# Routed experts on Trainium2: slots and ends formed by TensorE, rank rows for three experts, fetches by row block

## The reference, cut to what matters

```python
logits = xn @ router_weight.T + router_bias        # 8192 tokens, 16 experts
probs = softmax(logits, axis=-1)
_, idx = top_k(logits.T, 512)                      # each expert takes its 512 best tokens
xe = xn[idx]
h = gelu(einsum('ecd,efd->ecf', xe, fc1_weight) + fc1_bias[:, None, :])
y = einsum('ecf,edf->ecd', h, fc2_weight) + fc2_bias[:, None, :]
gates = take_along_axis(probs.T, idx, axis=1)
output = zeros.at[idx.reshape(-1)].add((y * gates[:, :, None]).reshape(-1, d))
```

## Time and profile before

| | |
|---|---|
| median of 3 runs | 966.09 us (965.4 to 966.34) |
| profiled execution | 965.09 us, span 963.4 us |
| mean granted clock of TensorE | 0.939 |
| PE busy | 855.3 us (89%), 6159 matmuls |
| DVE busy | 741.0 us (77%) |
| POOL busy | 593.4 us (62%) |
| ACT busy | 510.5 us (53%) |

### The profile page before, as it was taken

The page is one execution under the profiler, slowest core; times in us unless marked ns, Lnnn a source line. Parts: engine busy times, 40 slices in busy tenths (PEclk is TensorE's granted clock), DMA queues, the critical chain, the costliest instruction groups (busy, mean ns, idle before and its releaser), DMA issues. The chain is left out here.

```text
span 963.4 us, 21098 instructions
## 1 busy us (share of the span) xinstructions
PE 855.3 (89%) x6159; PEld 732.4 (76%) x6159; DVE 741.0 (77%) x1662; ACT 510.5 (53%) x929; POOL 593.4 (62%) x567
## 2 busy tenths in 40 slices
PE   8799999999999999999811159999999999999995
PEld 7678888788878887887611147989999999999985
DVE  4588888888888888887599766888777777777642
ACT  3456655665566556655366127465555555555541
POOL 4157666766676667665552356688877766775344
PEclk9899999999999999999855569999999999999998
DMA  5456665666566666654241033466665666665333
GB/s 174 153 196 202 217 215 201 206 214 222 198 201 218 211 201 207 219 200 150 86 146 44 14 103 122 157 176 174 167 166 158 162 160 163 166 173 147 93 71 44
DMA packets 129510, 156.51 MB, mean 162 GB/s; under 512 B 22449, under 2 KB 104625, under 8 KB 129345
## 3 DMA queue, kind: packets, MB, share of 16 engines
q1 hardware_dynamic: 104064, 113.05, 36.3%
q0 software_dynamic: 15616, 25.70, 12.5%
q10 hardware_dynamic: 9792, 17.31, 4.9%
HBM read 74.93 MB, written 26.28 MB: 105 GB/s over the span
## 5 line engine op out<-in xcount | busy, mean ns | idle before, releaser
L599 DVE TENSOR_REDUCE NM<-bank 128x4 f32<-128x480 f32 x256 | 155.5, 650 | 61.1 <-PE bank L761 61.0
L424 ACT ACTIVATE PT<-bank 120x512 f32<-120x512 f32 x256 | 142.5, 603 | 36.1 <-PE bank L786 34.9
L348 POOL TENSOR_SCALAR XN<-X,mv,rstd 128x256 f32<-128x256 f32 x124 | 150.5, 1222 | 14.1 <-POOL rstd L343 13.3
L1691 PE MATMUL bank<-W2H,HH 128*128 128x256 f32 x512 | 144.7, 283 | 2.0 <-issue 2.0
L1693 PE MATMUL bank<-W2H,HL 128*128 128x256 f32 x512 | 143.6, 280 | 0.0
L1692 PE MATMUL bank<-W2L,HH 128*128 128x256 f32 x512 | 143.5, 280 | 0.0
L1147 POOL DMA_INDIRECT out_dram<-C,IO x60 | 111.9, 1865 | 50.6 <-issue 31.3
L1417 DVE TENSOR_TENSOR HL<-hf,HH 128x512 fp32r<-128x512 f32 x128 | 87.3, 690 | 50.6 <-ACT HH L1572 49.9
L786 PE MATMUL bank<-QX,KX 128*120 128x256 f32 x512 | 110.6, 309 | 8.8 <-DMA QX<-NMT 5.2
L557 DVE RECIPROCAL RR<-RC 128x256 f32<-128x256 f32 x64 | 111.4, 1742 | 5.4 <-DMA RC<-PVS 5.3
L1567 ACT ACTIVATE hf<-bank,B 128x512 f32<-128x512 f32 x128 | 87.8, 686 | 41.4 <-PE bank L1693 35.5
(11 more groups left out here) (198 smaller groups left out, 1909.8 us busy)
## 6 DMA issues: line engine op xcount, KB each, us to landing
QX<-QH ACTq DMA_DIRECT2D x64, 256.0 KB
W<-w1T_dram SPq DMA_DIRECT2D x16, 1024.0 KB, 5.6
W<-w2T_dram SPq DMA_DIRECT2D x16, 1024.0 KB
X<-x_dram SPq DMA_DIRECT2D x32, 256.0 KB, 3.1
QX<-QL SPq DMA_DIRECT2D x32, 256.0 KB
XB<-x_dram SPq DMA_DIRECT2D x32, 256.0 KB, 2.9
RC<-PVS SPq DMA_DIRECT2D x64, 128.0 KB, 2.1
OC<-PVS SPq DMA_DIRECT2D x64, 128.0 KB, 2.2
```

Of the source, the lines that this page charges most:

```text
L348: ins = pool.tensor_scalar(dst[:, t, :], src[:, t, :], mv[:, t, 0:1], rstd[:, t:t + 1], ALU.subtract, ALU.mult)
L424: act.activation(PT[u][0:M, HE * k:HE * (k + 1), :], score_bank(b, k // 2)[k % 2][0:M, :], ACT.Exp, scale=SCALE) \
L599: dve.tensor_reduce(NM[u][:, t, :].rearrange("p (f n e) -> p n e f", n=HN, e=HE)[:, n, :, :], smax_bank[q % 2][:, 0:4 * M].rearrange("p (e ...
L1691: pe.matmul(o, wh, xh, start=first, stop=False)
```

## The change

TensorE now forms the ends of experts 2 to 15 by eight fp32 matmuls of a prefix column with the identity, and the slots (chosen and transposed in one) by sixteen: a prefix block times the identity, and the block shifted by one times its negative. prefix moves by one element in its tile, so that base, the value ahead of the first token, fits before it. Lines 1467 and 1468 and the larger spread_of go; minus_ident is new on POOL. FE is 3: expert 2's rank rows also come from first_ranks, and each store has its own semaphore. find_first and the first gathers work by halves of two row blocks. columns(0, 0) stands ahead of the counts of expert 1, tiles(1) ahead of those of expert 0, tiles(2) goes into the second loop of lows. The reciprocal moves behind spread_of. POOL's landed waits go, and its order becomes: first_lookup and first_gather of 0, 1, 2, first_rows 0, ranks(1, 1), first_rows 1, ranks(1, 0), gather(1, 1), ranks(2, 0).

The core of the diff (declarations, and what only renames, are left out):

```diff
@@ -1094,10 +1099,10 @@
         sp.wait_ge(prefix_ready, 1)
         for e in range(FE):
             sp.dma_start(first_ranks.rearrange("(e c j) p -> e c (j p)", e=FE, c=NC)[e], prefix[e:P:E, :]) \
-                .then_inc(first_stored, 16)
+                .then_inc(first_stored[e], 16)
         sp.wait_ge(table_ready, 1)
         rows = table_rows.rearrange("p j s q -> p (j s q)")
-        for e in (2, 0, 1, 3):
+        for e in range(4):
             sp.dma_start(slot_table.rearrange("(e c j) w -> e c (j w)", e=E, c=NC)[e], rows[e:P:E, :]).then_inc(early_stored, 16)
         for c in range(NC):
             sp.dma_start(slot_table.rearrange("(e c j) w -> c e (j w)", e=E, c=NC)[c, 4:E, :], rows[E * c + 4:E * (c + 1), :]) \
...
@@ -1171,32 +1177,34 @@
         pool.wait_ge(rsm_ready, 1)
         pool.tensor_tensor(probs[:, :, :], expl, rsm[:, :, :].to_broadcast([P, NT, E]), ALU.mult).then_inc(probs_ready, 1)
 
-        pool.wait_ge(first_stored, 16 * FE)
-        pool.wait_ge(row_ready, 1)
-
-        def landed(done, count):
-            pool.wait_ge(done, 16 * GT * count)
-
-        lookup(FR[0], first_ranks, row_of[:, 0, :], first_ranked[0])
-        lookup(FR[1], first_ranks, row_of[:, 1, :], first_ranked[1], range(GT // 2))
-        pool.wait_ge(idx_ready, 1)
-        lookup(XG[0], xn_table, II[0], gathered[0])
-        lookup(FR[1], first_ranks, row_of[:, 1, :], first_ranked[1], range(GT // 2, GT))
-        pool.wait_ge(idx_ready, 2)
-        lookup(XG[1], xn_table, II[1], gathered[1])
+        def first_lookup(e):
+            pool.wait_ge(first_stored[e], 16)
+            pool.wait_ge(row_ready, 1 + e // 2)
+            pool.wait_ge(idx_ready, e - 1) if e > 1 else None
+            for g in range(GT):
+                lookup(FR[e % 2], first_ranks, row_of[:, e, :], first_ranked[g], (g,))
+
+        def first_gather(e):
+            for half in range(2):
+                pool.wait_ge(half_found, 2 * e + half + 1)
+                if e == 2:
+                    pool.wait_ge(xt_done, 1)
+                lookup(XG[e % 2], xn_table, II[e % 2], gathered[e % 2], range(2 * half, 2 * half + 2))
+
+        first_lookup(0)
+        first_gather(0)
+        first_lookup(1)
+        first_gather(1)
+        first_lookup(2)
+        first_gather(2)
         pool.wait_ge(early_stored, 64)
-        pool.wait_ge(probs_ready, 1)
-        landed(gathered[1], 1)
+        lookup(first_rows[0], slot_table, row_of[:, 0, :], first_gated[0])
+        ranks(1, 1)
+        lookup(first_rows[1], slot_table, row_of[:, 1, :], first_gated[1])
         ranks(1, 0)
-        landed(ranked[0], 1)
-        lookup(first_rows[0], slot_table, row_of[:, 0, :], first_gated[0])
-        landed(first_gated[0], 1)
-        lookup(first_rows[1], slot_table, row_of[:, 1, :], first_gated[1])
-        gather(1, 0)
-        ranks(1, 1)
+        gather(1, 1)
         pool.wait_ge(slot_stored, 16 * NC)
         ranks(2, 0)
-        gather(1, 1)
         ranks(2, 1)
         add_up(0, 0, True)
         gather(2, 0)
...
@@ -1270,8 +1278,6 @@
                 decide(turn, r)
         decide(0, 30, True)
         n[0] = BASE + 2 * 31
-        dve.wait_ge(sum_ready, 4)
-        dve.reciprocal(rsm[:, :, :], tree[3]).then_inc(rsm_ready, 1)
         thr = cand[:, :].bitcast(FP32)
         dve.tensor_scalar(gt, LT, thr, None, ALU.is_gt, ALU.add, accum_out=counts[:, 0:1]).then_inc(step_dve, 1)
         dve.tensor_scalar(eq, LT, thr, None, ALU.is_equal, ALU.add, accum_out=counts[:, 1:2]).then_inc(step_dve, 1)
...
@@ -1284,6 +1290,7 @@
         dve.tensor_scalar(need[:, 4:5], need[:, 2:3], need[:, 0:1], float(CAP), ALU.subtract, ALU.add).then_inc(need_ready, 1)
         dve.tensor_tensor(need[:, 5:6], need[:, 2:3], need[:, 3:4], ALU.add).then_inc(need_ready, 1)
         dve.wait_ge(need_ready, 2)
+        dve.tensor_tensor(base, need[:, 5:6], need[:, 4:5], ALU.min)
         then(dve.tensor_tensor_scan(eq_count, eq, zero_row[:, :], need[:, 5:6], ALU.add, ALU.add))
         dve.scalar_tensor_tensor(prefix, eq_count, need[:, 4:5], gt_count, ALU.min, ALU.add).then_inc(prefix_ready, 1)
 
...
@@ -1294,8 +1301,13 @@
                               prefix[:, P - 1:CT:P].rearrange("p (a b j) -> p a b j", a=1, b=1).to_broadcast([P, hi - lo, NC, TC]),
                               ALU.mult).then_inc(spread_ready, 1)
 
-        def ends_of(lo, hi, src):
-            dve.tensor_copy(ends[:, lo:hi, :], src.rearrange("p (e t) -> p e t", t=NT)).then_inc(ends_ready, 1)
+        def first_ends():
+            dve.tensor_copy(ends[:, 0:2, :], first_ends_bank[:, 0:2 * NT].rearrange("p (e t) -> p e t", t=NT)).then_inc(ends_ready, 1)
+
+        def other_ends(k):
+            js = TC // 2
+            dve.tensor_copy(ends[:, 2:E, :].rearrange("p e (c j) -> p j e c", j=TC)[:, js * k:js * (k + 1), :, :].rearrange("p j e c -> p e c j"),
+                            ends_bank[k][:, 0:js * NC * (E - 2)].rearrange("p (j c e) -> p e c j", j=js, c=NC)).then_inc(ends_ready, 1)
 
         def tiles(g):
             lo, hi = GROUPS[g]
...
@@ -1357,11 +1369,19 @@
             dve.wait_ge(gate_picked, e + 1)
             dve.tensor_copy(all_gates[:, bass.ds(e, 1), :].rearrange("p o r -> p (o r)"), G[u][:, :]).then_inc(gate_found, 1)
 
-        def find_first(u):
-            dve.wait_ge(first_ranked[u], 16 * GT)
-            count(u, FR, first_place, range(GT))
-            dve.wait_ge(place_ready, u + 1)
-            numbers(u, u, first_place)
+        def find_first(e, half):
+            u, at, gs = e % 2, (first_place if e < 2 else place), slice(2 * half, 2 * half + 2)
+            for g in range(2 * half, 2 * half + 2):
+                dve.wait_ge(first_ranked[g], 16 * (e + 1))
+                ins = dve.tensor_scalar(before[:, g, :], FR[u][:, g, :], s_col[:, g:g + 1], None, ALU.is_le, ALU.add,
+                                        accum_out=at[u][:, g:g + 1])
+            ins.then_inc(half_counted, 1)
+            dve.wait_ge(half_counted, 2 * e + half + 1)
+            if e == 2:
+                dve.wait_ge(gathered[0], 16 * GT)
+            dve.scalar_tensor_tensor(II[u][:, gs], at[u][:, gs], float(NT), tile_of[:, e, gs], ALU.mult, ALU.add).then_inc(half_found, 1)
+            if half:
+                dve.scalar_tensor_tensor(out_row[:, e, :], tile_of[:, e, :], float(P), at[u][:, :], ALU.mult, ALU.add).then_inc(idx_ready, 1)
 
         def pick_first(u):
             dve.wait_ge(first_gated[u], 16 * GT)
...
@@ -1375,7 +1395,7 @@
             count(u, RK, place, (r,))
             if r == GT - 1:
                 dve.wait_ge(gathered[u], 16 * GT * i)
-                dve.wait_ge(place_ready, 2 * i + u + 1)
+                dve.wait_ge(place_ready, 2 * i + u - (FE - 1))
                 numbers(2 * i + u, u, place)
 
         def find_gates(i, u):
...
@@ -1460,37 +1480,40 @@
         dve.wait_ge(rank_consts, 5)
         dve.wait_ge(prefix_ready, 1)
         spread_of(0, 2)
+        dve.wait_ge(sum_ready, 4)
+        dve.reciprocal(rsm[:, :, :], tree[3]).then_inc(rsm_ready, 1)
         dve.wait_ge(ends_done, 1)
-        ends_of(0, 2, first_ends_bank[:, 0:2 * NT])
+        first_ends()
         dve.wait_ge(ends_ready, 1)
         tiles(0)
-        then(dve.scalar_tensor_tensor(eq, eq_count, need[:, 4:5], eq, ALU.is_le, ALU.mult))
-        dve.tensor_tensor(chosen, gt, eq, ALU.add).then_inc(chosen_ready, 1)
-        spread_of(2, E)
-        find_first(0)
-        gate_values()
         dve.wait_ge(ends_done, 2)
-        ends_of(2, 8, ends_bank[0][:, 0:6 * NT])
-        ends_of(8, 16, ends_bank[1][:, :])
+        other_ends(0)
+        other_ends(1)
         dve.wait_ge(ends_ready, 3)
         tiles(1)
+        find_first(0, 0)
+        find_first(0, 1)
+        gate_values()
         dve.wait_ge(row_ready, 2)
         next_rows(0, 0)
         next_rows(1, 1)
         dve.wait_ge(c_loaded, 32)
-        find_first(1)
         columns(0, 0)
+        find_first(1, 0)
+        find_first(1, 1)
         dve.wait_ge(table_ready, 1)
         dve.sem_inc(y0_ready, 1)
         for f in range(KF):
-            if f == 2:
-                tiles(2)
             if f == 5:
                 columns(0, 1)
             low(0, 0, f)
         for f in range(KF):
-            if f < GT:
-                find(1, 0, f)
+            if f == 1:
+                find_first(2, 0)
+            if f == 2:
+                find_first(2, 1)
+            if f == 4:
+                tiles(2)
             low(0, 1, f)
 
         split_1(2, 0)
...
@@ -1735,30 +1758,34 @@
 
         def keep_clock(times):
 
-
             for _ in range(times):
-                pe.matmul(first_ends_bank[:, :], ones16[:, :], spread[:, 8:16, :, :].rearrange("p e c j -> p (e c j)"), start=True, stop=True)
+                pe.matmul(first_ends_bank[:, :], W2H[:, 0, 0:P], W2H[:, 0:2, :].rearrange("p f d -> p (f d)"), start=True, stop=True)
 
         pe.wait_ge(rank_consts, 5)
         pe.wait_ge(spread_ready, 1)
```

(45 more changed lines are left out.)

## The result

The changed kernel takes 979.97 us, the median of 4 runs (979.51 to 984.07), beside 966.12 us (965.4 to 966.34, 4 runs) for the kernel before on the same chip. The ratio on record, with its 95% interval, is 1.0166 [1.0143, 1.0189]; that of the two medians alone is 1.0143. It is slower, by twice what was forecast (973), and 1 us above the range's end. The profiled execution took 980.08 us, its span 978.3; before, 965.09 and 963.4.

The account below looks back on a forecast made before the run. It took POOL's lookup order to set the pace, spending the 9.1 us early gain: up(1, 1) 5.5 us later plus 1.5 for the clock, 7.0 us on the median 966.09, giving 973, range 963.5 to 979.

Parts of the forecast that it names:

- rival 1: POOL does not set the pace: rows for find_gates(1, 0) land by 601.6, all 9.1 us stay, 957; chance 0.12.
- rival 2: Only the first wait: ranks(2, 0) land by 623.7, up(1, 1) starts at 636.1, about 967; chance 0.12.
- the forecast's 640.9: Forecast start of up(1, 1) on TensorE, behind late ranks(2, 0): 5.5 us later than before.
- the clock's 1.5: TensorE's second idle stretch, some 4 us, leaves its clock low: 1.5 us more (0 to 3).
- Tile rows: 545.44 - 0.37 = 545.07: At the search's end: tile rows ready at 545.07 instead of 545.44, with probs beside tiles(0) costing nothing.
- rival 3: Smaller early gain: probs hold tiles(0) 1.7 us, or slot matmuls run 2 us into gate values; 975 to 977; chance 0.14.
- The old one started 0.9 us after its row numbers were there, so it waited for the store of both ranks: POOL's first lookup: with one store releasing it, it starts at 545.35, a gain of 1.0 (bounds 0 and 1.0).
- rival 4: Lookups start no earlier, held by something else: up_1 stays, POOL's chain comes on top, above 980; chance 0.02.
- Its gathers land at 568.9, before TensorE asks at 569.3: Expert 1's gathers on POOL land before TensorE needs them, so up_1 starts at 576.7, 9.1 us earlier.
- The hold-ups on POOL: Lookups slowed beside DVE: 0.75 us beside W1L, and gather(1, 1)'s last held by W2L to 621.1, plus 0.94.
- the late landing: ranks(2, 0) land at some 630 instead of 628.6 if the W2 load that W2L releases is in the way.

Follow-up runs that it names:

- e4_recip: Changed kernel with the reciprocal back ahead of the two counts, so probs run during the search's end; ratio 1.0175 to the kernel before.
- e8_stores: Changed kernel with SP holding the eight later stores of slot_table until expert 1's gathers have landed; ratio 1.0162 to the kernel before.
- e1_swap: Changed kernel with POOL fetching expert 4's rank rows, ranks(2, 0), ahead of gather(1, 1), as before; ratio 1.0063 to the kernel before.
- e10_fe2_again: The same kernel as e6_fe2, run once more unchanged; ratio 0.9941 to the kernel before.
- e2_contrib: Changed kernel with contributions(0, 0) and split_2(1) right behind pick_first(0) on DVE; ratio 1.0172 to the kernel before.
- e3_early: Changed kernel with first_rows 0 and 1 and ranks(1, 0) on POOL ahead of expert 2's gathers; ratio 1.0067 to the kernel before.
- e6_fe2: Changed kernel with FE = 2: expert 2's rank rows from slot_table, POOL's order behind gather 1 as before, without landed waits; ratio 0.9943 to the kernel before.

## Why the prediction was half right

**The mechanism of the loss was right.** POOL does set the pace (rival 1 falls); it idles, then does 20 lookups without a gap; find_gates(1, 0), then W2L, are late; ranks(2, 0) behind gather(1, 1) make a second wait, and so rival 2 falls too. TensorE's new work is as costed: the ends 3.70 us (3.5), keep_clock(14) 3.45 (3.2 to 6.0), and the first product runs at 0.40 us a matmul. (1.97 / 8 is 0.25 and not 0.22 us, but the sixteen instructions of the ends took 0.23 each, so the slip cost nothing.)

**The size failed, at four terms;** three of them had a wait at nothing (1, 3) or laid it to the wrong cause (2). up(1, 1) is 7.3 us later than the forecast's 640.9, and the rest 0.65 us longer than the clock's 1.5.

1. *"Tile rows: 545.44 - 0.37 = 545.07"*: they came at 546.71, 1.64 late, 1.50 of it since probs hold the comparisons. This is rival 3, which got 0.14: the profile had no such pair, but e4_recip shows it. It is also the rule weighed there, that of the Trainium skill, SBUF — State Buffer, section "SBUF: two separate sides"; the trace agrees with it: 2.24 us beside probs, 0.74 without.
2. *"The old one started 0.9 us after its row numbers were there, so it waited for the store of both ranks"*: no. The lag is 0.92 in the changed kernel, which awaits one store, and 0.90 in e4_recip. So the second store isn't what it waits for; what it is stays open, as POOL's gather at 588.89 starts 0.27 us behind its numbers (588.46 + 0.16) and that at 621.22 0.84 behind out_row (620.38). I took a gain of 1.0, the upper bound; the start came 0.92 behind the row numbers instead of 0.28, so this term is 0.64 late. Both terms together are 2.28 of the 2.5 us by which up(0, 0) is late, at 564.90. The premise of rival 4, which got 0.02, came true: the first lookup starts at 547.63, before at 546.35. What rival 4 made of it did not: up_1 still came 2.9 us sooner than before.
3. *"Its gathers land at 568.9, before TensorE asks at 569.3"*: they start at 565.43 to 569.18 and land at 574.03. I put nothing on SP's stores of slot_table beside the gathers. Those stores hardly moved (the last eight start at 567.03 in the changed kernel), while the gathers came 2.2 us sooner, into them. The stores in the kernel before, whose last gather started at 571.37:

```profile
566.48 5.04 SPq L1103 DMA_DIRECT2D slot_table<-W  x8
```

The wait of 1.97 us and the slow matmuls behind it make up(0, 0) to up_1 18.0 us instead of 14.3, 3.7 late. Of the wait 1.1 us or more is the stores' (e8_stores); the slow matmuls are in part chance, since behind waits of 1.90 and 2.09 us at the same place e1_swap and e10_fe2_again kept their clock. So up_1 gained 2.9 and not 9.1.
4. *The hold-ups on POOL.* From its start on expert 2 to find_gates(1, 0) it took 28.24 us, not 27.0; and from there to find(2, 0, 0) 19.11, not 17.3, mostly since one gather was held for 4.22 us where I had some 2.9 (619.15 to 622.04): it ended 0.8 us behind W2L (2.28) and three low parts close behind it, 624.38 to 628.48. The rows also landed 2.89 us after the last start, not 2.45.

The 6.2 us that up_1 is late by reach POOL's start only as 4.6 (588.89 against 584.3: the first numbers of expert 2 come 6.0 us after up_1, not 7.6, as the matmuls behind up_1 kept their clock here and not in the kernel before). 4.59 + 1.24 + 1.81, less 0.38 for the steps from find(2, 0, 0) to up(1, 1) (11.92 instead of 12.3), is 7.26. The range's upper end held rival 3 or the late landing, not both; they aren't exclusive and should have been added.

## What to carry to other kernels

When a chain is made faster, ask of each engine in it whose program order puts work that is ready behind work that is not: here POOL stood idle 13.8 us ahead of expert 2's gathers, with twelve lookups behind them that needed none of their numbers. A wait that is taken away at one engine must be followed to the next thing that is late on another; e2_contrib took 9.4 us of idle away and gained nothing. Two engines' work that comes to stand side by side can cost time even where each has slack of its own, as probs beside the comparisons (1.5 us) and gathers beside SP's stores (1.1 us or more) did here, so bound such a pair from above before calling it covered.

## What the runs showed of the hardware that was not expected

- A lookup's descriptors can be held for the whole of several DVE operations in a row: the gather at 625.07 ends at 629.29, 0.8 us after the last of W2L and three low parts (628.48), where an undisturbed one takes 0.94. It starts 0.69 us into W2L; in e3_early, e4_recip and e8_stores one that starts 0.68 to 0.69 us into W2L takes 4.22 or 4.23 us too. The moment of the start goes with it: in the earlier trace rows the gather that starts 1.26 us into W2L takes 1.89 us and ends 0.8 behind W2L alone, though three low parts follow there as well. These are fp32 operations with two inputs in SBUF. The Trainium skill, SBUF — State Buffer, section "SBUF: two separate sides", names operations in a two-port mode as those that keep GpSimd from writing descriptors, and sets those with two SBUF inputs only against GpSimd operations that read SBUF; these traces show lookups held beside such operations, and not by what.
- After idle time of the same length TensorE's granted clock fell in one execution and stayed in another. Behind the wait of 1.99 us ahead of up_1 the matmuls ran 0.63 us each in the kernel before and 0.40 in the changed one, at 1.00 from 580 to 590. Of the twelve profiled executions here the clock fell at that place in eight, worth 1.6 us (12.6 us instead of 11.0 from up_1 to down(0, 0)). The wait of 1.99 us near the end of all of them does the same, in five of twelve; in e4_recip and in the changed kernel, by windows (the columns as in the earlier trace rows), that wait ends at 934.08 and at 936.45, and the stretch around it was granted 0.91 and 1.00:

```profile
920.00:940.00 20.00, 18.01 (x128) 17.14 (x128) 11.11 (x19) 4.94 (x6) 6.13 (x3) 0.91 0.30 73
```

```profile
920.00:940.00 20.00, 18.01 (x142) 17.14 (x141) 12.61 (x22) 7.32 (x10) 5.50 (x3) 1.00 0.22 46
```

The rest goes with it: 327.8 and 328.0 us where no stretch behind up(1, 1) is slow (e10_fe2_again, before), 329.5 with the end slow (e6_fe2), 330.1 with ten slow matmuls behind up(1, 1) (changed), 332.0 with both (e4_recip, e8_stores). So 1.6 to 2.2 us of a gain can come or go at each such place; what decides it isn't shown.
